# Scores of a cross-attention as three one-pass products of split operands, with the key side kept in parts for two groups of four batches and remade midway

## The chip, the cores and the metric

The kernel runs on one core of one Trainium2 chip. The metric is the time of one execution on the device in microseconds (us). Engines go by the profile's short names: PE (TensorE matmuls; PEld are its weight loads), DVE (VectorE), ACT (ScalarE), POOL (GpSimd), SP (SyncE, which issues most DMAs). A measurement of this kernel can tell about 0.2% from no change.

## The reference

One decoder layer on x of 16 batches x 256 rows x 128 features, with a context of 16 x 64 x 128. It has three parts, each followed by a residual sum and a layer norm. Cut to what matters:

```python
q, k, v = split_heads(x @ Wq + bq), ...            # 16 heads of 8
q = elu(q) + 1; k = elu(k) + 1
k = k / sqrt(sum(k * k, -1) + EPS)
attn = (q @ k^T) @ v                               # no softmax: linear
x = layernorm(x + layernorm(x + attn @ Wo + bo) * gamma + beta)

q, k, v = x @ Wq, context @ Wk, context @ Wv       # 16 heads of 64, 64 context rows
attn = softmax(q @ k^T / 8)
x = layernorm(x + (attn @ v) @ Wo)

h = silu(fp4(x) @ fp4(w_gate)^T) * (fp4(x) @ fp4(w_up)^T)   # fp4: blocks of 16, scaled to their maximum
x = layernorm(x + fp4(h) @ fp4(w_down)^T)
```

## The kernel before

**Work and tiles.** A batch is two tiles of 128 rows. For every batch the kernel runs a front (the linear attention and its two norms, which give `x1`), a cross-attention of two tiles, and an FFN. The wide intermediate results are in PSUM, whose eight banks of 512 floats a partition are shared out as `A1` and `A2` (one bank each) and `S`, `TP`, `F` (two each).

**Scores.** The query and key weights are folded: for each head h, G_h = Wk_h Wq_h^T, and M_h = G_h^T ctx^T, so that the scores of a tile are x1 M. G is made at the start and split into a part rounded to fewer bits and the rest (`GT[:, 0]` and `GT[:, 1]`, of type fp32r, which PE takes in one pass). The context is split likewise (`ctx_r`). The upper part of a split is cut with a bit mask on DVE (`context_cut`, `g_cut_high`, `gate_up_cut`, `xf_cut_high`), copied to fp32r by ACT, and the rest is a subtraction. M of all 16 heads and all 16 batches is then made in the head of the program, as 32 head products (16 heads x two halves of the batches, `m_product`) of three fp32r matmuls of 512 columns each, and kept as plain fp32 by ACT and DVE in turns (`m_keep`). The scores of a tile (`scores`) are two fp32 matmuls of 512 columns; the compiler makes two instructions of every fp32 matmul, so a tile has four.

**A tile's way.** `S` holds a tile's scores: `score_max` (DVE) takes the maxima of 16 heads, `scores_shift` (PE) subtracts them by a matmul, `softmax_exp` (ACT) writes `pe`; POOL folds halves and later multiplies by the reciprocal sums; `p_transpose` and `values` (PE) fill `TP`, ACT copies it to SBUF, and `cross_out` uses it. `x1_transpose` writes the transposed `x1` into `S` too, and `keep_x1T` (ACT) copies it out before the scores. `h_transpose` of the FFN also uses `TP`.

**Order.** There is no scheduler at run time. Each engine has its own list of calls, written out, which it takes strictly in order; semaphores hold an instruction until what it needs is there or its buffer is free. DVE's list begins with biases, masks and splits; the FFN weights are quantised in the head (`weights_max` to `weights_dequantised`, DVE) and transposed by PE (`weights_transpose`).

The products that the change is about read so in the kernel before:

```python
for n, (left, right) in enumerate(PARTS):          # m_product: 3 parts
    te.matmul(m_bank(half, hd), GT[:, left, hd, :], ctx_r[:, right, 512 * half:512 * half + 512], ...)
for half in range(2):                              # scores
    te.matmul(S[:, half * BANK:half * BANK + BANK], x1T[b % 2][:, t * P:t * P + P],
              M[:, b // BH, HC * half:HC * half + HC, b % BH * R:b % BH * R + R], ...)
```

Of the kernel before, what the change touches and what calls it, by code (L numbers as in the profile page):

```python
# [17 lines left out]
def decoder_layer(nc, x, x_t, attn_w, attn_rows, ctx_t, wq_t, wk_t, wv_t, wo_in, fw_in, out):  # L18
# [17 lines left out]
    BH = B // 2  # L36
# [22 lines left out]
    with es:  # L59
# [35 lines left out]
        M = sb("M", [P, 2, HX, BH * R])  # L95
# [12 lines left out]


        m_tail = M[:, 1, :, :].rearrange("p h n -> p (h n)")  # L110
        fw, fw_v, fw_c = (m_tail[:, HX * BH * R - (k + 1) * NW:HX * BH * R - k * NW] for k in range(3))

# [14 lines left out]
        pe_ = several("pe", NPE, [P, HX * R])  # L127
        xv = several("xv", 2, [P, T * P])
        th = sb("th", [P, T, I])
        hv = several("hv", 2, [P, T * I])  # L130
# [11 lines left out]
        x1T = several("x1T", 2, [P, T * P])  # L142
# [7 lines left out]
        xf_cut = sb("xf_cut", [P, T * P])  # L150

        xf_r = [GT[:, k, 0:2 * T, :].rearrange("p (s t) n -> p s (t n)", s=2) for k in range(2)]
# [3 lines left out]
        hT = several("hT", 2, [P, T, NK * P])  # L156
# [10 lines left out]
        fw_m, fw_s, fw_r = (hT[1][:, 0, NWB * k:NWB * k + NWB] for k in range(3))  # L167
        gu_cut = [w[:, 1, 0:I] for w in hT]

        high_bits = [w[:, 512 * k:512 * k + 512] for w in pe_ for k in range(2)]  # L170
# [37 lines left out]
        c_cut, c_high, c_low = sem("c_cut"), sem("c_high"), sem("c_low")  # L208
        g_made, g_cut, g_high, g_low = sem("g_made"), sem("g_cut"), sem("g_high"), sem("g_low")
        m_made = sem("m_made")  # L210
        m_kept = {"act": sem("m_kept_act"), "dve": sem("m_kept_dve")}
# [15 lines left out]
        x1T_made, x1T_kept, vo_made, vo_kept = sem("x1T_made"), sem("x1T_kept"), sem("vo_made"), sem("vo_kept")  # L227
# [7 lines left out]
        xf_cut_made, xf_low_made = sem("xf_cut_made"), sem("xf_low_made")  # L235
        gu_cut_made, gu_high_made, gu_low_made = sem("gu_cut_made"), sem("gu_high_made"), sem("gu_low_made")
# [15 lines left out]
        DN_OF = (A2, A1) if TILE_SUM_ON_PE else (A2, A2)  # L252
# [36 lines left out]
        M_BANKS = (F0, F1, TP0, TP1, S0, S1)  # L289

        def m_bank(half, hd):
            return M_BANKS[(HX * half + hd) % len(M_BANKS)]

# [3 lines left out]
        def _(sp):  # L297
# [27 lines left out]
            load_xT(2)  # L325
            load_x(2)
            load_xT(3)
            load_x(3)
            load_xT(4)
# [6 lines left out]
            load_x(8)  # L336
            load_xT(7)
            load_xT(8)
            load_xT(9)
            load_x(9)  # L340
            load_x(10)
            load_x(11)
            load_xT(10)
            load_xT(11)
            load_x(12)
            store_out(0)
            store_out(1)
            load_xT(12)
            load_x(13)
            store_out(2)  # L350
            load_x(14)
            load_xT(13)
            load_xT(14)
            store_out(3)
            load_x(15)
            load_xT(15)
            store_out(4)
            store_out(5)
            store_out(6)
# [9 lines left out]
            store_tile(15, 1)  # L369
            for n in range(2):  # L370
                sp.wait_ge(out_stored[n], 16 * (B // 2 + n))

        @block.gpsimd
        def _(pool):
# [28 lines left out]
            def context_low(half):  # L403
                pool.wait_ge(c_cut, half + 1)
                cols = slice(512 * half, 512 * half + 512)
                ge.tensor_tensor(ctx_r[:, 1, cols], ctx_f[:, cols], high_bits[half], ALU.subtract).then_inc(c_low, 1)

            def gate_up_low(m):
                pool.wait_ge(gu_cut_made, m + 1)
                ge.tensor_tensor(w_gu_r[:, 1, m, :], w_gu[:, m, :], gu_cut[m], ALU.subtract).then_inc(gu_low_made, 1)  # L410
# [107 lines left out]

            context_low(0)
# [3 lines left out]
            k_norm(0)  # L523
            gate_up_low(0)
            gate_up_low(1)
            minus_mean("attn", 0)
            variance_eps("attn", 0)
            rstd_of("attn", 0)
            shift_of("attn", 0)
            times_gamma(0)  # L530
            plus_x_beta(0)
            k_norm(1)
            x_plus_rows(2)
            variance_eps("post", 0)
            minus_mean("post", 0)
            rstd_of("post", 0)
            shift_of("post", 0)
            k_norm(2)
            variance_eps("attn", 1)
            minus_mean("attn", 1)  # L540
            rstd_of("attn", 1)
            shift_of("attn", 1)
# [3 lines left out]
            fold_halves(0, 0)  # L546
            minus_mean("post", 1)
            variance_eps("post", 1)
            k_norm(3)
            rstd_of("post", 1)  # L550
            shift_of("post", 1)
            probabilities(0, 0)
            variance_eps("attn", 2)
            fold_halves(0, 1)
            minus_mean("attn", 2)
            rstd_of("attn", 2)
            shift_of("attn", 2)
            probabilities(0, 1)
            times_gamma(2)
            plus_x_beta(2)  # L560
            x_plus_rows(4)
            minus_mean("post", 2)
            variance_eps("post", 2)
            fold_halves(1, 0)
            rstd_of("post", 2)
            k_norm(4)
            shift_of("post", 2)
            probabilities(1, 0)
            fold_halves(1, 1)
            variance_eps("cross", 0)  # L570
            rstd_of("cross", 0)
            minus_mean("cross", 0)
            shift_of("cross", 0)
            probabilities(1, 1)
            k_norm(5)
            fold_halves(2, 0)
            x_dequantise(0)
            variance_eps("cross", 1)
            minus_mean("cross", 1)
            rstd_of("cross", 1)  # L580
            shift_of("cross", 1)
            probabilities(2, 0)
            k_norm(6)
            fold_halves(2, 1)
            variance_eps("attn", 3)
# [3101 lines left out]
```

## Time and profile before

| | us |
|---|---|
| median of 3 runs (lowest, highest) | 372.77 (372.73, 373.13) |
| span of the profiled execution | 371.1 |
| PE busy | 349.7 (94%) |
| DVE busy | 308.7 (83%) |
| ACT busy | 253.6 (68%) |
| POOL busy | 269.0 (73%) |

The profiled execution has a span, from its first to its last instruction, of 371.1 us; the runs' median lies 1.7 us above it, which is what lies around the span. Busy time is the time in which an engine runs at least one instruction. PE's matmuls overlap at their ends, so the pace of a kind of matmul is read from the distance between the ends of successive groups, not from the mean duration of one.

### The profile page before, as it was taken

To read this page: it belongs to the slowest core of one execution; us is meant where nothing else is said; L and a number is where in the kernel's file an instruction comes from. 1 tells how busy PE (TensorE), PEld (TensorE's weight loads), DVE (VectorE), ACT (ScalarE), POOL (GpSimd) and SP (SyncE) were. 2 spreads that over 40 slices of the span, in tenths; PEclk is the share of its full clock that TensorE was granted. 3 is DMA by queue.
4 is the path that set the end of the run, shared out by engine and by line. 5 is a ranking of instruction groups with operands and counts; after the bars stand their busy time and mean duration, and the time that the engine had idled before them with its cause. 6 is when DMAs were issued, how large, how long until landed. Compare 5 with 4: busy or idle time off the path is not lost.

```text
span 371.1 us, 7329 instructions
## 1 busy us (share of the span) xinstructions
PE 349.7 (94%) x2147; PEld 267.9 (72%) x2147; DVE 308.7 (83%) x858; ACT 253.6 (68%) x533; POOL 269.0 (73%) x453
## 2 busy tenths in 40 slices
PE   8999989999998999999999999999999999998774
PEld 7788646675775868787678877786767787887653
DVE  3998557567689998869989779979998998999994
ACT  2957766577676677678688767878767666864553
POOL 4404459958988699969689895898988569784535
PEclk9999999999999999999999999999999999999999
DMA  8900100001000001000000000100000000000010
GB/s 248 305 2 16 30 1 16 14 16 29 15 17 14 17 0 44 28 18 16 29 14 17 14 1 17 31 0 0 17 15 2 15 2 1 15 16 14 3 30 28
DMA packets 13586, 10.44 MB, mean 28 GB/s; under 512 B 971, under 2 KB 12396, under 8 KB 13548
## 3 DMA queue, kind: packets, MB, share of 16 engines
q1 hardware_dynamic: 12540, 7.89, 7.1%
q10 hardware_dynamic: 1008, 2.10, 1.7%
q8 instruction: 18, 0.29, 0.3%
q14 instruction: 20, 0.16, 0.1%
HBM read 7.88 MB, written 2.10 MB: 27 GB/s over the span
## 4 chain that ended last, share of the span: by engine, by line
PE 70%; DVE 9%; POOL 8%; issue 6%; ACT 4%; DMA 1%; SPq 0%; POOLq 0%; DVEq 0%
PE A L2892 13%; PE S L2862 12%; PE TP L2852 7%; PE F L2916 6%; PE TP L2880 6%; PE A L2936 5%; PE S L2871 3%; PE A L2813 2%; PE TP L2791 2%; POOL pe L440 2%; PE F L2791 2%; PE S L2791 2%; PE TP L2925 2%; PE A L2826 2%; PE A L2821 1%
## 5 line engine op out<-in xcount | busy, mean ns | idle before, releaser
L440 POOL TENSOR_TENSOR pe<-pe,srec 128x1024 f32<-128x1024 f32 x32 | 60.9, 1904 | 9.2 <-DVE srec L1860 8.9
L2862 PE MATMUL S<-M,x1T 128*128 128x512 f32 x128 | 60.7, 597 | 1.5 <-ACT pe L1076 1.4
L2892 PEld LDWEIGHTS A<-wvoT,wqkT 128*128 128x128 f32 x480 | 56.4, 192 | 3.1 <-issue 1.8
L2892 PE MATMUL A<-wvoT,wqkT 128*128 128x128 f32 x480 | 58.0, 276 | 0.1
L434 POOL TENSOR_TENSOR fold<-pe 128x512 f32<-128x512 f32 x32 | 40.9, 1277 | 14.6 <-ACT pe L1076 14.4
L1843 DVE TENSOR_REDUCE smax<-S 128x16 fp32r<-128x1024 f32 x32 | 38.7, 1211 | 3.3 <-PE S L2862 3.1
L1076 ACT ACTIVATE pe<-S 128x1024 f32<-128x1024 f32 x32 | 32.6, 1019 | 10.6 <-PE S L2871 10.3
L1081 ACT ACTIVATE wqkT<-TP 128x1024 f32<-128x1024 f32 x32 | 32.6, 1018 | 4.3 <-PE TP L2880 4.1
L2862 PEld LDWEIGHTS S<-M,x1T 128*128 128x128 f32 x128 | 22.2, 190 | 18.3 <-issue 15.3
L2916 PE MATMUL F<-w_gu_r,GT 128*128 128x352 f32 x168 | 35.1, 344 | 0.1
L2880 PE MATMUL TP<-ident,pe 128*128 128x128 f32 x256 | 33.5, 274 | 1.6 <-POOL pe L440 0.9
L2880 PEld LDWEIGHTS TP<-ident,pe 128*128 128x128 f32 x256 | 28.8, 140 | 6.2 <-issue 3.0
L2852 PE MATMUL TP<-HW,ctx_f 128*64 128x512 f32 x128 | 31.0, 605 | 0.0
L2916 PEld LDWEIGHTS F<-w_gu_r,GT 128*128 128x128 f32 x168 | 26.9, 189 | 4.4 <-issue 3.2
L2936 PEld LDWEIGHTS A<-w_dn,hT 128*128 128x128 f32 x180 | 21.5, 192 | 6.6 <-issue 4.7
L450 POOL TENSOR_TENSOR hv<-hv,ham 128x704 f32<-128x704 f32 x15 | 20.8, 1389 | 6.1 <-DVE hv L1935 5.9
L1854 DVE TENSOR_REDUCE ssum<-fold 128x16 f32<-128x512 f32 x32 | 21.7, 677 | 4.3 <-POOL fold L434 4.2
L2936 PE MATMUL A<-w_dn,hT 128*128 128x128 f32 x180 | 23.0, 277 | 2.0 <-ACT hT L1105 2.0
L425 POOL TENSOR_TENSOR kn<-fk,ky 128x256 f32<-128x256 f32 x16 | 10.1, 631 | 20.0 <-DVE ky L1808 19.9
L418 POOL TENSOR_TENSOR xb<-x_sb,rows 128x512 f32<-128x512 f32 x16 | 20.3, 1274 | 4.2 <-DMA rows<-in_attn_rows 3.0
L2871 PE MATMUL S<-smax,ident_r 128*128 128x512 f32 x64 | 21.8, 422 | 1.7 <-DVE smax L1843 1.7
L1070 ACT ACTIVATE wvoT<-TP 128x1024 f32<-128x1024 f32 x16 | 16.4, 1022 | 6.8 <-PE TP L2852 6.8
(247 smaller groups left out, 888.2 us busy)
## 6 DMA issues: line engine op xcount, KB each, us to landing
xT<-in_x_t SPq DMA_DIRECT2D x16, 128.0 KB, 2.2
x_sb<-in_x SPq DMA_DIRECT2D x16, 128.0 KB, 2.2
out<-yf SPq DMA_DIRECT2D x15, 128.0 KB, 1.8
M<-in_fw SPq DMA_DIRECT2D x1, 560.0 KB, 11.0
wqkT<-in_wq_t ACTq DMA_DIRECT2D x2, 256.0 KB, 4.6
wqkT<-in_wk_t ACTq DMA_DIRECT2D x2, 256.0 KB, 6.1
ctx_f<-in_ctx_t ACTq DMA_DIRECT2D x2, 256.0 KB, 7.0
wvoT<-in_wv_t ACTq DMA_DIRECT2D x1, 512.0 KB, 9.4
```

Source lines behind the costliest of these rows:

```text
L434: ge.tensor_tensor(by_head(fold[n % NFO][:, :]), p4[:, :, 0, :], p4[:, :, 1, :], ALU.add).then_inc(fold_made, 1)
L440: ge.tensor_tensor(w, w, spread(srec[n % NFO][:, :], HX, R), ALU.mult).then_inc(pn_made, 1)
L1076: sc.activation(pe_[n % NPE][:, :], S[:, :], ACT.Exp, scale=SCALE).then_inc(pe_made, 1)
L1081: sc.activation(pT[n % 2], TP[:, :].rearrange("p (a n) -> p a n", a=NJ), ACT.Copy).then_inc(pT_kept, 1)
L1843: ve.tensor_reduce(smax[n % 2][:, :], by_head(S[:, :]), AX.X, ALU.max, negate=True).then_inc(smax_made, 1)
L2852: last = te.matmul(TP[par * R:par * R + R, half * BANK:half * BANK + BANK], ctx_f[:, b * R:b * R + R], HW[:, par, 4 * half:4 * half + 4, : ...
L2862: last = te.matmul(S[:, half * BANK:half * BANK + BANK], x1T[b % 2][:, t * P:t * P + P], M[:, b // BH, HC * half:HC * half + HC, b % BH * ...
L2871: last = te.matmul(S[:, half * BANK:half * BANK + BANK], ident_r[:, :], spread(smax[n % 2][:, HC * half:HC * half + HC], HC, R), start=Fal ...
L2880: last = te.transpose(TP[:, j * P:j * P + P], pe_[n % NPE][:, j * P:j * P + P], ident[:, :])
L2892: last = te.matmul(part(A2, t), pT[n % 2][:, j, :], vo[b % 2][:, j, :], start=(j == 0 and b not in SUM_ON_PE), stop=(j == NJ - 1))
L2916: last = te.matmul(bk[:, 0:I], part(xf_r[b % 2][:, left, :], t), w_gu_r[:, right, m, :], start=(n == 0), stop=(n == len(PARTS) - 1))
L2936: last = te.matmul(part(DN, t), hT[b % 2][:, t, k * P:k * P + P], w_dn[:, k, :], start=(k == 0 and b not in SUM_ON_PE), stop=(k == NK - 1))
```

## The change

The scores become three fp32r products per half tile instead of one fp32 product. For this x1T is split into two fp32r parts: `keep_x1T` (ACT) now rounds into the first, and a new `x1T_keep_low` (DVE) writes the rest, from `S`. M is kept as two fp32r parts as well: `m_keep_high` (ACT) and `m_keep_low` (DVE). That doubles its bytes, so M holds only two groups of four batches at a time; groups 0 and 1 are made in the head, groups 2 and 3 later, over the places of groups 0 and 1, once the scores of those are done. A group is made in four quarters of four heads: 12 matmuls of 256 columns fill two banks, and one copy and one subtraction of 1024 columns empty them. The bit masks are gone: the rounded copy by ACT is itself subtracted. The FFN weights' work space moves from `M` to `pe`, `hv`, `hT` and `th`. `xf_r` gets its own buffers. All lists are written anew; at the end of PE's list the filling matmuls that write nothing of use (`keep_warm`) go from 18 to 24.

```diff
-        M = sb("M", [P, 2, HX, BH * R])
+        M = sb("M", [P, 2, 2, HX, BG * R], FP32R)
...
-        x1T = several("x1T", 2, [P, T * P])
+        x1T = several("x1T", 2, [P, 2, T * P], FP32R)
...
-        M_BANKS = (F0, F1, TP0, TP1, S0, S1)
+        M_BANKS = (TP, S, F, S, F, TP, S, F) + (TP,) * 8
...
             def g_keep_high(half, par):
-                k = 2 * half + par
-                act.wait_ge(g_cut, k + 1)
-                sc.activation(g_tile(half, par)[0], high_bits[2 + k].rearrange("p (a b) -> p a b", a=4),
+                act.wait_ge(g_made, half + 1)
+                sc.activation(g_tile(half, par)[0], G_BANKS[half][par].rearrange("p (a b) -> p a b", a=4),
                               ACT.Copy).then_inc(g_high, 1)
...
-            def m_keep(half, hd):
-                act.wait_ge(m_made, HX * half + hd + 1)
-                if half == 1 and hd >= 9:
-                    act.wait_ge(fwT_made, 3)
-                sc.activation(M[:, half, hd, :], m_bank(half, hd), ACT.Copy).then_inc(m_kept["act"], 1)
+            def m_keep_high(g, q):
+                act.wait_ge(m_made, NQ * g + q + 1)
+                if g >= 2:
+                    act.wait_ge(s_made, T * BG * (g - 1))
+                sc.activation(m_part(g, q, 0), m_bank(g, q), ACT.Copy).then_inc(m_high, 1)
...
+            def m_keep_low(g, q):
+                dve.wait_ge(m_high, NQ * g + q + 1)
+                ve.tensor_tensor(m_part(g, q, 1), m_bank(g, q), m_part(g, q, 0).bitcast(FP32), ALU.subtract).then_inc(m_low, 1)
+
+            def x1T_keep_low(b):
+                dve.wait_ge(x1T_kept, b + 1)
+                ve.tensor_tensor(x1T[b % 2][:, 1, :], S[:, 0:T * P], x1T[b % 2][:, 0, :].bitcast(FP32), ALU.subtract).then_inc(x1T_low, 1)
...
-            def xf_cut_high(b):
...
             def xf_keep_low(b):
-                dve.wait_ge(xf_cut_made, b + 1)
-                ve.tensor_tensor(xf_r[b % 2][:, 1, :], A2[:, 0:T * P], xf_cut[:, :], ALU.subtract).then_inc(xf_low_made, 1)
+                dve.wait_ge(xfT_kept, b + 1)
+                ve.tensor_tensor(xf_r[b % 2][:, 1, :], A2[:, 0:T * P], xf_r[b % 2][:, 0, :].bitcast(FP32),
+                                 ALU.subtract).then_inc(xf_low_made, 1)
...
+            def m_product(g, q):
+                k = 2 * (q // 2) + 2
+                pe.wait_ge(g_high, k)
+                pe.wait_ge(g_low, k)
+                pe.wait_ge(c_high, g // 2 + 1)
+                pe.wait_ge(c_low, g // 2 + 1)
+                for a in range(QH):
+                    for n, (left, right) in enumerate(PARTS):
+                        last = te.matmul(m_bank(g, q)[:, a, :], GT[:, left, QH * q + a, :], ctx_r[:, right, BG * R * g:BG * R * g + BG * R],
+                                         start=(n == 0), stop=(n == len(PARTS) - 1))
                 last.then_inc(m_made, 1)
...
             def scores(b, t):
+                g = b // BG
                 pe.wait_ge(x1T_kept, b + 1)
-                if b % BH == 0 and t == 0:
-                    pe.wait_ge(m_kept["act"], HC * (b // BH + 1))
-                    pe.wait_ge(m_kept["dve"], HC * (b // BH + 1))
-                for half in range(2):
-                    last = te.matmul(S[:, half * BANK:half * BANK + BANK], x1T[b % 2][:, t * P:t * P + P],
-                                     M[:, b // BH, HC * half:HC * half + HC, b % BH * R:b % BH * R + R],
-                                     start=True, stop=True)
+                pe.wait_ge(x1T_low, b + 1)
+                if b % BG == 0 and t == 0:
+                    pe.wait_ge(m_high, NQ * g + NQ)
+                    pe.wait_ge(m_low, NQ * g + NQ)
+                for n, (left, right) in enumerate(PARTS):
+                    for half in range(2):
+                        last = te.matmul(S[:, half * BANK:half * BANK + BANK], part(x1T[b % 2][:, left, :], t),
+                                         M[:, g % 2, right, HC * half:HC * half + HC, b % BG * R:b % BG * R + R],
+                                         start=(n == 0), stop=(n == len(PARTS) - 1))
                 last.then_inc(s_made, 1)
```

**PE in the head.** Before, PE's list in the head is mainly products of M (`ctx_r,GT`), between which single steps of batch 0's front and the transposes of the FFN weights (`F<-ident,M`) stand:

```order
L2791 MATMUL TP<-ctx_r,GT 128x512 x6
L2799 MATMUL F<-ident,M 128x128 x3
L2791 MATMUL S<-ctx_r,GT 128x512 x3
L2826 MATMUL A<-kn,vals 128x128 x2
L2799 MATMUL F<-ident,M 128x128 x3
L2791 MATMUL S<-ctx_r,GT 128x512 x3
L2831 MATMUL A<-w_attn,kvT 128x128
```

In the changed kernel batch 0's front up to its output (`kvo,fq`) stands ahead of the first quarter of M (the row of 12):

```order
L2755 MATMUL TP<-wqkT 128x128 x8
L2806 MATMUL A<-xT,w_attn 128x256
L2811 MATMUL A<-kn,vals 128x128 x2
L2816 MATMUL A<-w_attn,kvT 128x128
L2806 MATMUL A<-xT,w_attn 128x256
L2822 MATMUL A<-kvo,fq 128x128 x2
L2776 MATMUL TP<-ctx_r,GT 128x256 x12
```

What moved: the front of batch 0 went from amid the products of M to before them, and eight quarters are left in the head of what were 32 head products.

**PE at the first quarter that is remade.** Before, PE's list in the scores of batch 4 goes from tile to tile (`S<-smax` is the shift, `TP<-ident,pe` a transposed tile, `w_gu_r` the FFN's first products):

```order
L2862 MATMUL S<-M,x1T 128x512 x2
L2899 MATMUL A<-ident,xv 128x128 x2
L2871 MATMUL S<-smax,ident_r 128x512 x2
L2880 MATMUL TP<-ident,pe 128x128 x8
L2862 MATMUL S<-M,x1T 128x512 x2
```

After the change, the second scores of batch 3 (the last that read group 0) are followed by the first quarter of group 2, in `TP`:

```order
L2850 MATMUL S<-M,x1T 128x512 x6
L2806 MATMUL A<-xT,w_attn 128x256
L2904 MATMUL F<-w_gu_r,xf_r 128x352 x6
L2776 MATMUL TP<-ctx_r,GT 128x256 x12
L2811 MATMUL A<-kn,vals 128x128 x2
L2859 MATMUL S<-smax,ident_r 128x512 x2
L2796 MATMUL A<-kv_bias_r,ones_r 128x256
L2798 MATMUL A<-w_attn,xT 128x256
```

What is new: the scores have six instructions instead of four half as fast ones, and quarters of M take turns in `TP` with `values`, the transposed tiles and the FFN's transposes. Until the next row that writes `TP` (the second quarter) there stand the rows shown here, one more pair of the last two, a `w_attn,kvT` and an `x1_transpose`.

**DVE ahead of the first maximum.** In the changed kernel the subtraction for x1T stands in DVE's list eight rows ahead of the first maximum (`smax`), with steps of other batches' fronts and a copy of `HW` (a folded value weight) between:

```order
L1737 TENSOR_TENSOR x1T<-S,x1T 128x256
L1789 TENSOR_REDUCE kss<-ksq 128x32
L1741 COPY HW<-TP 128x512
L1794 TENSOR_SCALAR ky<-A 128x32
L1832 BN_AGGR mv_attn<-stats_attn 128x2
L1833 BN_AGGR mv_attn<-stats_attn 128x2
L1799 TENSOR_TENSOR kh<-kyy,A 128x32
L1803 SCALAR_TENSOR_TENSOR ky<-A,ky 128x32
L1838 TENSOR_REDUCE smax<-S 128x16
```

Behind DVE's second maximum (of batch 0's second tile) the new list has less of the fronts left than the old one: 10 instead of 11 `fk`, 11 instead of 13 `fq`, 22 instead of 24 of each of `kh` and the later `ky`, 12 instead of 13 `kvT`, 13 instead of 14 `x<-A,xb` with their statistics. It has new there: 8 `M<-TP` and 14 `x1T<-S`; and it lacks 15 `xf_cut`.

## Rows read from the trace of the kernel before

**Rows 1.** The page: span, busy time of each engine (share) and instructions.

```profile
span 371.1 us, 7329 instructions
PE 349.7 (94%) x2147; PEld 267.9 (72%) x2147; DVE 308.7 (83%) x858; ACT 253.6 (68%) x533; POOL 269.0 (73%) x453
```

**Rows 2.** Windows: stretch, its length, busy us of each engine (instructions), clock, DMA.

```profile
0.00:58.44 58.44, 54.38 (x296) 40.39 (x296) 42.30 (x106) 36.87 (x89) 24.20 (x56) 1.00 0.31 98
...
120.00:240.00 120.00, 119.30 (x757) 92.20 (x757) 105.28 (x298) 88.53 (x184) 97.96 (x154) 1.00 0.06 19
240.00:330.00 90.00, 88.78 (x568) 69.35 (x568) 82.00 (x229) 63.12 (x125) 74.80 (x128) 1.00 0.03 9
330.00:371.10 41.10, 29.23 (x204) 25.13 (x202) 34.32 (x93) 20.64 (x42) 20.24 (x43) 0.99 0.06 17
```

**Rows 3.** The page: shares of the chain that ended last, by engine and line.

```profile
PE 70%; DVE 9%; POOL 8%; issue 6%; ACT 4%; DMA 1%; SPq 0%; POOLq 0%; DVEq 0%
PE A L2892 13%; PE S L2862 12%; PE TP L2852 7%; PE F L2916 6%; PE TP L2880 6%; PE A L2936 5%; PE S L2871 3%; PE A L2813 2%; PE TP L2791 2%; POOL pe L440 2%; PE F L2791 2%; PE S L2791 2%; PE TP L2925 2%; PE A L2826 2%; PE A L2821 1%
```

**Rows 4.** Timeline of PE: start, us, instruction, count; cross-attention output and scores.

```profile
149.80 0.60 PE L2880 MATMUL TP<-ident,pe 128*128 128x128 f32 x4
150.24 3.74 PE L2892 MATMUL A<-wvoT,wqkT 128*128 128x128 f32 x32
153.81 1.88 PE L2862 MATMUL S<-M,x1T 128*128 128x512 f32 x4
```

**Rows 5.** Timeline of PE in the head: products of M, and a bias product.

```profile
18.62 0.59 PE L2813 MATMUL A<-w_attn,xT 128*128 128x256 f32 x2
18.86 0.47 PE L2811 MATMUL A<-kv_bias_r,ones_r 128*128 128x256 f32 x1
...
25.08 1.52 PE L2791 MATMUL S<-ctx_r,GT 128*128 128x512 f32 x6
26.44 1.52 PE L2791 MATMUL F<-ctx_r,GT 128*128 128x512 f32 x6
```

**Rows 6.** PEld by line: busy, mean ns of one load, idle before.

```profile
L2791 PEld LDWEIGHTS F<-ctx_r,GT 128*128 128x128 f32 x36 | 6.5, 188 | 1.4 <-DVE GT L1730 0.2
```

**Rows 7.** DVE and ACT by line: busy us, mean ns, idle before and its releaser.

```profile
L1843 DVE TENSOR_REDUCE smax<-S 128x16 fp32r<-128x1024 f32 x32 | 38.7, 1211 | 3.3 <-PE S L2862 3.1
...
L1896 DVE TENSOR_SCALAR xf_cut<-A 128x256 int32<-128x256 int32 x15 | 6.2, 414 | 1.4 <-PE A L2899 1.2
...
L1901 DVE TENSOR_TENSOR GT<-A,xf_cut 128x256 fp32r<-128x256 f32 x15 | 6.2, 411 | 0.2
...
L1737 DVE COPY M<-F 128x512 f32<-128x512 f32 x6 | 4.1, 675 | 0.6 <-PE F L2791 0.4 <-PE F L2801 0.2
...
L1724 DVE TENSOR_SCALAR pe<-F 128x512 int32<-128x512 int32 x2 | 1.3, 682 | 0.0
L1081 ACT ACTIVATE wqkT<-TP 128x1024 f32<-128x1024 f32 x32 | 32.6, 1018 | 4.3 <-PE TP L2880 4.1
...
L974 ACT ACTIVATE M<-F 128x512 f32<-128x512 f32 x6 | 3.5, 590 | 0.8 <-PE F L2791 0.8
```

**Rows 8.** Timeline: DVE's first step on data, and the first scores to the second shift.

```profile
6.39 0.15 DVE L1704 TENSOR_SCALAR bq_col<-w_attn 128x1 f32<-128x1 f32 x1 [5.26 <-DMA rows<-in_attn_rows]
...
50.12 1.88 PE L2862 MATMUL S<-M,x1T 128*128 128x512 f32 x4
52.04 1.22 DVE L1843 TENSOR_REDUCE smax<-S 128x16 fp32r<-128x1024 f32 x1 [0.34 <-PE S L2862]
53.32 0.70 PE L2871 MATMUL S<-smax,ident_r 128*128 128x512 f32 x2 [0.20 <-DVE smax L1843]
54.06 1.02 ACT L1076 ACTIVATE pe<-S 128x1024 f32<-128x1024 f32 x1 [1.59 <-PE S L2871]
58.44 0.70 PE L2871 MATMUL S<-smax,ident_r 128*128 128x512 f32 x2
```

More of the change, by code:

```diff
@@ L358, in _ @@
             store_out(5)
+            load_x(15)
             store_out(6)
@@ new lines, in _ @@
+            project_q(3)
+            pe.wait_ge(ky_made, 9)
+            kv_outer(2)
+            pe.wait_ge(m_low, 4)
+            m_product(1, 2)
+            kv_project(2)
+            attn_out(2)
+            pe.wait_ge(fq_made, 4)
+            project_kv(4)
+            pe.wait_ge(m_low, 5)
+            m_product(1, 3)
+            pe.wait_ge(m_low, 7)
+            x1_transpose(0)
+            pe.wait_ge(m_low, 6)
+            hw_product(1)
+            pe.wait_ge(fk_made, 5)
+            project_q(4)
@@ L3084, in _ @@
+            scores(0, 0)
+            values(0)
+            scores_shift(0, 0)
+            pe.wait_ge(ky_made, 15)
+            kv_outer(3)
+            pe.wait_ge(fq_made, 5)
+            project_kv(5)
+            pe.wait_ge(pe_made, 1)
+            x1_transpose(1)
+            kv_project(3)
             pe.wait_ge(vo_kept, 1)
             values(1)
-            pe.wait_ge(ky_made, 9)
-            attn_out(1)
-            pe.wait_ge(m_kept["act"], 15)
-            pe.wait_ge(m_kept["dve"], 15)
@@ L3273, in _ @@
+            h_transpose(2)
             pe.wait_ge(yx_made, 6)
-            project_q(8)
-            pe.wait_ge(pT_kept, 12)
-            values(7)
-            pe.wait_ge(xg_made, 5)
-            kv_outer(8)
-            pe.wait_ge(fq_made, 9)
-            xf_transpose(3)
-            scores_shift(6, 0)
-            pe.wait_ge(vo_kept, 8)
-            h_transpose(2)
-            kv_project(8)
+            project_kv(10)
+            pe.wait_ge(pe_made, 13)
+            scores(6, 1)
             pe.wait_ge(hg4_made, 3)
@@ L3297, in _ @@
-            pe.wait_ge(ya_made, 9)
-            kv_outer(9)
+            values(6)
+            scores(7, 0)
+            pe.wait_ge(fk_made, 12)
+            project_q(9)
             pe.wait_ge(h_made, 7)
             gate_up(3, 1)
-            pe.wait_ge(pe_made, 14)
-            x1_transpose(7)
+            pe.wait_ge(vo_kept, 7)
+            values(7)
+            pe.wait_ge(xg_made, 6)
+            attn_out(9)
+            scores_shift(7, 0)
+            pe.wait_ge(vo_kept, 8)
+            p_transpose(6, 0)
@@ L3392, in _ @@
-            pe.wait_ge(ky_made, 39)
-            kv_outer(11)
+            pe.wait_ge(fk_made, 14)
+            down(4)
             pe.wait_ge(h_made, 13)
             gate_up(6, 1)
-            kv_project(11)
+            pe.wait_ge(yf_made, 5)
+            project_q(11)
+            pe.wait_ge(hT_kept, 5)
+            values(10)
             pe.wait_ge(pe_made, 20)
             x1_transpose(10)
-            pe.wait_ge(fk_made, 14)
+            pe.wait_ge(ky_made, 42)
+            attn_out(11)
@@ L3450, in _ @@
             pe.wait_ge(pT_kept, 22)
-            values(12)
-            pe.wait_ge(pe_made, 22)
-            x1_transpose(11)
+            h_transpose(6)
+            pe.wait_ge(pe_made, 23)
+            scores(11, 1)
             pe.wait_ge(yx_made, 11)
             down(6)
-            pe.wait_ge(x1T_kept, 12)
-            scores(11, 0)
-            pe.wait_ge(ky_made, 45)
-            kv_project(13)
+            pe.wait_ge(xg_made, 9)
+            kv_outer(14)
+            scores_shift(11, 1)
@@ L3477, in _ @@
             pe.wait_ge(hT_kept, 8)
             p_transpose(11, 0)
[L3479 to L3489 removed]
+            attn_out(14)
+            scores_shift(12, 0)
+            pe.wait_ge(xf_low_made, 10)
@@ L3512, in _ @@
-            pe.wait_ge(xf_low_made, 10)
-            down(8)
-            pe.wait_ge(x1T_kept, 14)
-            scores(13, 0)
+            pe.wait_ge(pT_kept, 24)
+            h_transpose(8)
+            scores(13, 0)
+            pe.wait_ge(h_made, 19)
+            gate_up(9, 1)
+            pe.wait_ge(hT_kept, 9)
+            values(13)
+            scores_shift(13, 0)
+            pe.wait_ge(fq_made, 16)
+            down(8)
+            pe.wait_ge(xg_made, 11)
+            kv_outer(15)
+            pe.wait_ge(vo_kept, 14)
```

3062 lines of the change are left out of this document (1474 added, 1588 removed).

## The prediction

> **What bounds the kernel now.** Begin with the busy times [rows 1]: PE is busy for 349.7 of 371.1 us, and DVE, the next, for 308.7. The chain of waits that ended last runs through PE for 70% of the span, and the scores are its second largest line with 12% [rows 3]. A mean over the whole program hides stages, so the windows come next [rows 2]. From 120 to 330 us PE is busy for 208.1 of 210 us: there its work is the time. DVE is busy for 88% of the one stretch and 91% of the other, so it is close behind. In the head, up to the second shift of the scores at 58.44 us, PE is busy for 54.4 us and DVE for 42.3. In the last 41.1 us PE is busy for 29.2, DVE for 34.3: the tail is a chain of steps of the last batches, in which PE has idle time. So what PE saves counts fully in the middle, only as far as DVE follows in the head, and little in the tail.
>
> **The pace of each matmul** is read from the ends of successive rows. The four instructions of a tile's scores end at 155.69 (153.81 + 1.88); the row ahead of them ended at 153.98: 1.71 us [rows 4]. Six fp32r products of 512 columns end at 27.96, the six before at 26.60: 1.36 us, 0.227 each [rows 5]. For 256 columns there is no row of many; one such product ends at 19.33, 0.12 behind its forerunner's 19.21 [rows 5]. Its bounds: below, 0.112, the pace of the 32 instructions that end at 153.98 after 150.40 [rows 4]; above, 0.188, the duration of one weight load [rows 6], if a row of 12 products went at the pace of its loads. I take 0.12, since loads as long stand in the 32 that go at 0.112.
>
> **PE's account.** A tile's scores fall from 1.71 to 1.36 us; 32 tiles give back 11.2. M's products were 96 x 0.227 = 21.8 us and become 192 x 0.12 = 23.0, so 1.2 more. The sum is 10.0 us less on PE. The six extra `keep_warm` matmuls (1.3 us) lie in the tail's idle time; with no idle they would cost that.
>
> Where it falls: half of M (11.5 us) is now made in the middle. So the head loses 21.8 - 11.5 = 10.3 for M and 0.7 for its two tiles. It gains about one batch's front, which the new order draws forward: two `project_q` (0.43 each, half of half a tile's fp32 scores), and at 0.112 four instructions each of `kv_outer` and `attn_out` and two of `kv_project`, together 2.0. The head thus has 9.0 us less for PE; the rest has 30 x 0.35 = 10.5 less for scores, 11.5 more for M, 2.0 less of front: 1.0 less.
>
> **DVE's account.** Removed are 16 copies of M at 0.675 (10.8), 15 FFN masks at 0.414 (6.2) and eight masks in the head, six of 512 columns at 0.68 and two smaller, about 5.0 [rows 7]. Added are 16 subtractions of 1024 columns for M and 16 of 256 for x1T. The second kind is the same operation as L1901, 0.411 each, 6.6 in all. For the first no row exists; the nearest, by size and bank, is the maximum over 1024 columns, 1.21, and two copies of 512, 1.35, bound it above [rows 7]. I take 1.21: 19.4. The net is 4.0 more. Behind the second shift it is 8 x 1.21 + 14 x 0.411 - 6.2 and less one front of some 15 short steps (about 4, an estimate from steps of 0.15 to 0.5): 5.3 more. In the head it is 1.3 less, so 41.0. ACT gets 16 copies of 1.02 for 16 of 0.59, 6.9 more [rows 7]; at 68% busy it has the room. POOL's and SP's work stays as it is; the FFN weights only land in another tile.
>
> **The head, step by step.** With 9.0 us less PE would be busy for 45.4 us. DVE begins at 6.39 [rows 8] and needs 41.0: it can't reach its second maximum's end before 47.4. It had 9.8 us idle between 6.39 and 58.44, in which it waited for ACT and PE; if it keeps all of that, the second shift starts at 57.2. Part of it stays, since the rsqrt steps of the fronts (`kh`, `ky`) go to and fro between ACT and DVE whatever PE does, and new waits come: a quarter of M goes PE, ACT, DVE, and x1T waits for ACT and then DVE. Behind `x1T_keep_low` in DVE's queue stand `kss`, `HW`, a `ky` chain and the maximum, so a late `keep_x1T` holds all those, and then PE's shift and ACT's exponential. I take the middle, 53.0: **5.4 us less**, with bounds of 1.2 and 11.0.
>
> **The rest.** PE has 1.0 us less. Each remade quarter holds `TP` until ACT's copy (1.02) and DVE's subtraction (1.21) are through. Three hand-overs come to it, each 0.05: PE's scores end at 52.00, the maximum starts at 52.04 and ends at 53.26, the shift starts at 53.32 and ends at 54.02, the exponential starts at 54.06 [rows 8]. Six products last 1.52 at a pace of 1.36 [rows 5], so the last is ready 0.16 late. Together 2.54 us. What PE has to do meanwhile, behind the first of them: `kv_outer` 0.45, the shift 0.45, `project_kv` 1.10, `kv_project` 0.22, the transposes 0.22, together 2.44. So 0.1 is missing; for eight quarters I take **1.2**, with bounds of nothing and of 9.7 (DVE comes one 1.21 us step late each time, as its list is strictly in order). DVE's 5.3 us more I cost at nothing: from 240 to 330 it is 91% busy while PE stands still for only 1.2 of 90 us [rows 2], and 5.3 over some 310 us lifts its share by under 2%. DVE also has 13 steps more behind its last maximum; that work has moved from before it and adds nothing to the sum, but the last scores must come earlier by as much.
>
> **The sum.** 371.1 - 5.4 - 1.0 + 1.2 = 365.9 us of span. The runs' median lies 1.7 above the profiled span, so 367.6.
>
> **Rivals.**
> *PE's saving in full.* If DVE's waits in the head go with PE's work, all 10.0 us come out: 361.1 + 1.7 = 362.8. For it speaks the middle, where PE alone decides; against it that the head would be DVE's at 47.4 without a single wait.
> *Given back.* DVE keeps its waits in the head (1.2 gained), the remade quarters cost 1.2, and a quarter of DVE's 5.3 us more shows in the rest (1.3): 371.1 - 1.2 - 1.0 + 1.2 + 1.3 = 371.4, so 373.1, no change. DVE's 91% speaks for it, PE's nearly idle-free middle at that share against it.
> *Slower by the remade quarters.* Place: `m_keep_low` of groups 2 and 3 in DVE's list. If DVE gets there one long step late each time, PE waits ahead of the next writer of `TP`, and the transposed tiles, `values` and `h_transpose` behind it. At 9.7 us the sum is 371.1 - 5.4 - 1.0 + 9.7 = 374.4, so 376.1; from 0.8 us a quarter on it is slower than before. For it: the cover is 0.1 short already. Against: only eight places.
> *Slower by weight loads.* The 192 products of 256 columns go at the loads' 0.188: 13.1 us more, of which the head's half finds PE's idle time but for 0.5. The result is 367.6 + 0.5 + 6.5 = 374.6. Against it stands that 32 instructions, each with a load, ended every 0.112 us [rows 4]. The Trainium skill, "TensorE: Matmul & The Clock Gate", Part 3, states that a weight load overlaps running matmuls only where it targets another group of rows, which would put every load beside its product. By that rule this case would be the likely one, and 374.6 its least time; the trace of these full 128-row loads doesn't agree, as products of 0.227 with loads of 0.188 between them leave no room for it.
>
> **Chances and range.** The forecast, with 365 to 370.5 as its own range: 0.50. The full saving: 0.24. Given back: 0.12. The remade quarters: 0.11. The loads: 0.03. Leaving out the far ends of the first and the fourth, 361.5 to 374 remains. What a measurement can tell from no change is about 0.2%, 0.7 us. Of "given back" some 0.03 falls below that; so faster 0.77, same 0.09, slower 0.14.
>
> **What would show it.** Right, if six score products end 1.36 us apart from the row ahead, 12 of M take 1.4 to 1.5, `M<-TP` on DVE has a mean near 1.21, and the second shift starts at 51 to 55 us. The first step falls if that shift stands past 57 or before 50. The second falls if PE idles ahead of rows that write `TP`, released by DVE's `M`, for more than 3 us in all. The forecast is wrong altogether if PE's busy share in the middle drops below 96%, since DVE's load was then not free.

## The result and the profile after

The changed kernel takes 360.97 us (median of five runs, 360.79 to 362.69), against 372.94 for the kernel before beside it: a ratio of 0.969 [0.9672, 0.9708], 12.0 us less. In a second comparison it took 361.1 us, ratio 0.9685 [0.9669, 0.9702]. The forecast was 367.6 with a range from 361.5: the kernel is faster than the range allowed.

It was profiled twice. The first profiled execution (span 360.9) was the longest of its five; the others have spans of 359.0 to 359.5. The second has 359.4, like these, and its rows are read here. First the page's busy times and the shares of the chain that ended last, for [rows 1, 3]:

```profile
span 359.4 us, 7621 instructions
...
PE 340.4 (95%) x2319; PEld 286.7 (80%) x2319; DVE 307.9 (86%) x851; ACT 255.9 (71%) x533; POOL 272.1 (76%) x453
...
PE 35%; POOL 25%; issue 22%; DVE 11%; ACT 4%; DMA 1%; POOLq 0%; ACTq 0%; DVEq 0%
```

Next the windows of the same execution, cut at its own second and last shift of the scores (53.68 and 314.77), for [rows 2]:

```profile
0.00:53.68 53.68, 45.55 (x315) 37.28 (x316) 41.65 (x107) 38.89 (x93) 30.79 (x62) 1.00 0.35 111
53.68:120.00 66.32, 65.75 (x435) 54.40 (x434) 51.13 (x158) 48.89 (x105) 58.94 (x90) 1.00 0.05 15
120.00:240.00 120.00, 119.16 (x808) 100.48 (x806) 106.71 (x295) 90.24 (x185) 92.39 (x144) 1.00 0.05 15
240.00:314.77 74.77, 74.77 (x529) 65.03 (x527) 70.03 (x189) 54.81 (x104) 65.51 (x110) 1.00 0.04 10
314.77:359.40 44.63, 35.18 (x243) 29.50 (x241) 38.39 (x106) 23.05 (x47) 24.52 (x51) 0.97 0.07 21
```

PE is busy for 45.55 us of the head; the forecast said 45.4. The middle looks as full as before. Where the time went is read from the shifts on PE's timeline. The first fence is of the kernel before (its second shift, at 58.44, stands in [rows 8]), the other of the changed kernel:

```profile
330.02 0.60 PE L2871 MATMUL S<-smax,ident_r 128*128 128x512 f32 x2
```

```profile
50.71 1.65 PE L2850 MATMUL S<-M,x1T 128*128 128x512 f32 x6 [0.70 <-DVE x1T L1737]
...
53.68 0.70 PE L2859 MATMUL S<-smax,ident_r 128*128 128x512 f32 x2
...
314.77 0.68 PE L2859 MATMUL S<-smax,ident_r 128*128 128x512 f32 x2
```

| stretch | before, us | after, us | difference | forecast |
|---|---|---|---|---|
| start to second shift | 58.4 | 53.7 | -4.7 | -5.4 |
| second to last shift | 271.6 | 261.1 | -10.5 | |
| last shift to end | 41.1 | 44.6 | +3.5 | |
| both behind the second shift | 312.7 | 305.7 | -7.0 | +0.2 |

The head came nearly as forecast. The miss lies behind it: 7.0 us less where nothing was expected. What went is read from windows: first of the kernel before (the row that [rows 2] leave out, and the whole stretch behind the second shift), then of the changed kernel:

```profile
58.44:120.00 61.56, 58.03 (x328) 40.84 (x329) 44.80 (x136) 44.46 (x96) 51.85 (x75) 1.00 0.06 16
...
58.44:371.10 312.66, 295.34 (x1852) 227.53 (x1852) 266.40 (x753) 216.76 (x445) 244.85 (x397) 1.00 0.05 15
```

```profile
53.68:359.40 305.72, 294.86 (x2006) 249.40 (x2004) 266.26 (x745) 216.99 (x441) 241.36 (x392) 0.99 0.05 15
```

PE is busy there for 0.5 us less (295.3 to 294.9). Its idle time, the stretch less the busy time, fell by 6.5 (17.32 to 10.86):

| PE's idle time | before, us | after, us |
|---|---|---|
| second shift to 120 us | 3.5 | 0.6 |
| 120 us to last shift | 1.9 | 0.8 |
| last shift to end | 11.9 | 9.4 |
| together | 17.3 | 10.9 |

### The profile page after: what moved, and what is told of

It is laid out like the page before. It is cut to its first block, busy times and chain, and to the rows that moved or that the text cites. A ratio compares the mean times of both kernels' runs of the same rounds, so it can differ in the third digit from the quotient of the medians.

```text
span 360.9 us, 7621 instructions
## 1 busy us (share of the span) xinstructions
PE 342.2 (95%) x2319; PEld 288.1 (80%) x2319; DVE 307.8 (85%) x851; ACT 256.0 (71%) x533; POOL 271.8 (75%) x453
## 4 chain that ended last, share of the span: by engine, by line
PE 52%; POOL 16%; issue 14%; DVE 11%; ACT 4%; DMA 1%; POOLq 0%; ACTq 0%; DVEq 0%
PE A L2880 11%; PE S L2850 8%; PE TP L2837 5%; PE TP L2868 5%; PE F L2904 4%; POOL pe L445 3%; PE A L2798 3%; PE A L2924 2%; PE S L2859 2%; POOL fold L439 2%; PE TP L2776 2%; POOL hv L455 2%; DVE smax L1838 2%; PE TP L2913 2%; DMA wqkT<-in_wk_t 1%
## 5 line engine op out<-in xcount | busy, mean ns | idle before, releaser
L2850 PE MATMUL S<-M,x1T 128*128 128x512 f32 x192 | 52.8, 410 | 0.7 <-DVE x1T L1737 0.7
L439 POOL TENSOR_TENSOR fold<-pe 128x512 f32<-128x512 f32 x32 | 42.1, 1314 | 12.6 <-ACT pe L1081 12.4
L2850 PEld LDWEIGHTS S<-M,x1T 128*128 128x128 f32 x192 | 34.0, 189 | 10.4 <-issue 1.8
L1086 ACT ACTIVATE wqkT<-TP 128x1024 f32<-128x1024 f32 x32 | 32.7, 1021 | 10.9 <-PE TP L2868 10.8
L2904 PE MATMUL F<-w_gu_r,xf_r 128*128 128x352 f32 x168 | 33.9, 337 | 0.1
L2904 PEld LDWEIGHTS F<-w_gu_r,xf_r 128*128 128x128 f32 x168 | 27.4, 188 | 1.4 <-DVE h L1899 0.5
L1849 DVE TENSOR_REDUCE ssum<-fold 128x16 f32<-128x512 f32 x32 | 21.3, 672 | 6.1 <-POOL fold L439 6.0
L430 POOL TENSOR_TENSOR kn<-fk,ky 128x256 f32<-128x256 f32 x16 | 11.1, 696 | 16.9 <-DVE ky L1803 16.7
L2859 PE MATMUL S<-smax,ident_r 128*128 128x512 f32 x64 | 21.4, 416 | 0.7 <-DVE smax L1838 0.7
```

The source lines that it names most:

```text
L439: ge.tensor_tensor(by_head(fold[n % NFO][:, :]), p4[:, :, 0, :], p4[:, :, 1, :], ALU.add).then_inc(fold_made, 1)
L1086: sc.activation(pT[n % 2], TP[:, :].rearrange("p (a n) -> p a n", a=NJ), ACT.Copy).then_inc(pT_kept, 1)
L2850: last = te.matmul(S[:, half * BANK:half * BANK + BANK], part(x1T[b % 2][:, left, :], t), M[:, g % 2, right, HC * half:HC * half + HC, b % ...
L2859: last = te.matmul(S[:, half * BANK:half * BANK + BANK], ident_r[:, :], spread(smax[n % 2][:, HC * half:HC * half + HC], HC, R), start=Fal ...
L2904: last = te.matmul(bk[:, 0:I], part(xf_r[b % 2][:, left, :], t), w_gu_r[:, right, m, :], start=(n == 0), stop=(n == len(PARTS) - 1))
```

## Experiments

Each kernel was run in three rounds beside the kernel before (372.65 to 372.99 in these comparisons). Differences below are from the before of the same comparison. Theory A is that PE's work decides and what it saves counts in full. Theory B is that each engine's strictly ordered list is fitted to durations, that a chain of hand-overs runs right behind PE, and that the new lists made the gain.

**1. The new products in the old lists.** x1's second part is subtracted on DVE (16 times); the part of M that doesn't fit is read from other heads' places.

```diff
+            x1T_keep_low(0)
...
+                pe.wait_ge(x1T_low, transposed[0])
+                for n, (left, right) in enumerate(PARTS):
+                    for half in range(2):
+                        last = te.matmul(S[:, half * BANK:half * BANK + BANK], part(x1T[b % 2][:, left, :], t),
...
+                                         start=(n == 0), stop=(n == len(PARTS) - 1))
-                for half in range(2):
-                    last = te.matmul(S[:, half * BANK:half * BANK + BANK], x1T[b % 2][:, t * P:t * P + P],
```

> The lists of before, with the scores as three one-pass products and x1T's subtraction put into DVE's list where ACT's copy of x1T had ended in the trace of before. M is rounded to one part and made whole in the head as before; the scores take its upper part twice (M's rest is left out), and for the second eight batches heads 9 to 15 are read from other heads' places. Theory A (the gain is PE's work, every us of it, and DVE's 6.6 us more are free): 32 x 0.35 = 11.2 us less, 361.7 us. Theory B (the new lists are what saved waits; old lists can't use the shorter scores): 365 us or more. Theory C (shorter scores take waits away too, as the way of a tile through S gets shorter): 360 us or less.

372.35 us, 0.9993 [0.9984, 1.0003]: no gain that can be told from none, as Theory B expected. Its page's busy times, its chain, and two of PE's waits:

```profile
PE 345.5 (93%) x2211; PEld 280.3 (76%) x2211; DVE 311.7 (84%) x874; ACT 254.2 (69%) x533; POOL 269.6 (73%) x453
...
POOL 37%; issue 24%; PE 21%; DVE 13%; ACT 3%; POOLq 1%; DVEq 0%; ACTq 0%
```

```profile
PE S L2900 <- DVE smax L1851: 2.9, 6, 1.1
...
PE S L2891 <- DVE x1T L1846: 1.6, 5, 0.6
```

By the forecast's paces PE has 11.2 us less to do, but its busy time fell by only 4.2 (349.7 to 345.5) and the time by 0.3. PE fell out of the chain (70% to 21%): it now waits for the others. Its idle time rose by 3.9 (21.4 to 25.3); the other 7 us of the 10.9 that it waits longer don't show as idle time.

**2. The old products in the new lists.** The subtractions for the second parts still run.

```diff
-                for n, (left, right) in enumerate(PARTS):
-                    for half in range(2):
-                        last = te.matmul(S[:, half * BANK:half * BANK + BANK], part(x1T[b % 2][:, left, :], t),
-                                         M[:, g % 2, right, HC * half:HC * half + HC, b % BG * R:b % BG * R + R],
...
+                for half in range(2):
+                    last = te.matmul(S[:, half * BANK:half * BANK + BANK], part(x1T[b % 2][:, 0, :], t),
+                                     M[:, g % 2, 0, HC * half:HC * half + HC, b % BG * R:b % BG * R + R],
```

> The changed kernel with its own lists, M and x1T kept as plain fp32 copies, and the scores again one fp32 product of four instructions; DVE's subtractions still run (they write zeros that nothing reads). Theory A: 11.2 us more than the changed kernel, 372.2 us. Theory B: less than 11.2 more, 368 us or less, since the new lists have waits in which PE's extra work fits. Theory C: more than 11.2, 374 us or more.

370.64 us, 0.9946 [0.9931, 0.9960]: 9.7 above the changed kernel, between Theories A and B and nearer A. Here the same 11.2 us of PE's work count almost fully.

**3. The new lists without the remade quarters.** The eight quarters of groups 2 and 3 are left out, and those groups' scores read the M of groups 0 and 1.

```diff
-            m_product(2, 0)
...
-            m_keep_high(2, 0)
...
-            m_keep_low(2, 0)
```

> The changed kernel without the eight remade quarters: products, copies and subtractions of groups 2 and 3 are left out, and batches 8 to 15 take their scores from the M of batches 0 to 7. PE has 96 products of 256 columns less, 11.6 us; DVE 9.7 us less, ACT 8.2 less. Theory A: 349.4 us. If the quarters also made PE wait for TP (the recorded forecast took 1.2 us for it): 348 us. If DVE was a bound in the middle after all: below 347 us.

358.28 us, 0.9613 [0.9599, 0.9628], 2.7 less than the changed kernel: all three expectations fail. By the rows' paces PE has 11.5 us less to do, DVE 9.8, ACT 8.2. But behind the second shift PE now stands idle for 18.7 us instead of 10.9. Taking work out of lists that were written for it frees little, as in experiment 1, so this run doesn't show what the quarters cost where they stand.

**4. Only the FFN mask left out of the kernel before.**

```diff
-            xf_cut_high(0)
...
-                dve.wait_ge(xf_cut_made, b + 1)
-                ve.tensor_tensor(xf_r[b % 2][:, 1, :], A2[:, 0:T * P], xf_cut[:, :], ALU.subtract).then_inc(xf_low_made, 1)
+                dve.wait_ge(xfT_kept, b + 1)
+                ve.tensor_tensor(xf_r[b % 2][:, 1, :], A2[:, 0:T * P], xf_r[b % 2][:, 0, :].bitcast(FP32),
+                                 ALU.subtract).then_inc(xf_low_made, 1)
```

> The kernel before with one part of the change alone: the FFN's mask on DVE is gone, ACT rounds straight from PSUM and DVE subtracts that. DVE has 15 x 0.414 = 6.2 us less, and its subtraction now waits for ACT's copy. Theory A: no change, 372.9 us within 0.7. If DVE's load was a bound in the old lists: 2 to 6 us less. If the wait for ACT holds up what is queued behind it: 1 to 3 us more.

377.01 us, 1.0114 [1.0097, 1.0131]: DVE is busy for 5.4 us less and the kernel is 4.4 us slower, more than the third expectation's 1 to 3. DVE's largest wait is one that the kernel before doesn't have, for ACT's copy of the same 256 columns:

```profile
DVE GT L1895 <- ACT GT L1093: 12.0, 13, 1.9
```

**5. The same, with the subtraction one to six steps later in DVE's list**, in twelve of 15 batches (its expectation counts eleven and five).

```diff
-            xf_keep_low(0)
             score_max(3, 0)
+            xf_keep_low(0)
```

> The kernel before without the FFN mask (which alone gave 377.0, with 12.0 us of DVE's waiting for ACT at the subtraction of 256 columns behind it), and with that subtraction moved back in DVE's list by one to five steps in eleven of 15 batches, so that the steps behind it need not wait. If the 4.4 us came from its place in the list: 371.5 to 373.5, so the loss goes. If they came from the longer way of the FFN's input itself (PE, ACT, then DVE): 375.5 to 378.

384.17 us, 1.03 [1.0271, 1.0329], 11.3 us slower than the kernel before: both expectations fail. DVE's wait fell from 12.0 to 1.1, but PE's FFN products now wait for DVE:

```profile
PE F L2896 <- DVE GT L1895: 6.9, 4, 1.7
```

Neither the old place nor these later ones suit the step. Whether it would be free if its neighbours on PE and ACT moved too was not tried.

**6 and 7. POOL's longest step halved**, with the old and with the new products in the old lists; **8, below,** does it in the changed kernel.

```diff
-                w = by_head(pe_[n % NPE][:, :])
-                ge.tensor_tensor(w, w, spread(srec[n % NFO][:, :], HX, R), ALU.mult)
+                w = by_head(pe_[n % NPE][:, :])[:, 0:HX // 2, :]
+                ge.tensor_tensor(w, w, spread(srec[n % NFO][:, 0:HX // 2], HX // 2, R), ALU.mult)
```

> The kernel before, with the multiplication of the probabilities (POOL, 1.90 us, 32 times) done on half of its columns only; the other half stays without its division, so the output isn't the reference's. POOL has about 30 us less, and each tile's probabilities come some 0.95 us sooner. Theory A (PE's work is the time of this kernel, POOL has slack): no change, 372 to 373. Theory B (a chain through POOL, DVE and ACT stands right behind PE): little or no change here either, since PE's 349.7 us of work stay; at most 2 us less. A fall of 5 us or more would say that PE's 70% of the chain of waits was misleading in the kernel before.

> The lists of before with the new products of the scores (which alone gave 372.35) and with POOL's multiplication of the probabilities on half of its columns, as in the run beside it. Theory B1 (the 11.3 us that PE saves were lost to the chain of hand-overs in which POOL has 37%): with POOL's step shorter a good part of the saving shows, 363 to 367. Theory B2 (the old lists themselves hold it, each engine waiting at places that POOL does not decide): 370 to 373, as with POOL's full step. Theory A expects what it expected of the new products alone, about 362.

372.33 us (0.9982 [0.9972, 0.9991]) and 370.22 us (0.9928 [0.9913, 0.9943]). POOL's busy time falls by 27 us in both (269.6 to 242.2 in the second), and the second gains 2.3 on experiment 1, relative to its own before. The first is what Theories A and B both expected. The second lies in the range of B2, and B1 fails: POOL's 37% of the chain are not a price, and this step of POOL is not what holds most of the saving.

**8.** 

> The changed kernel with POOL's multiplication of the probabilities on half of its columns (as done with the lists of before, where it gave 0.5 us with the old products and 2.1 with the new). If POOL's chain (16% of the chain of waits after the change) is what the changed kernel is next held by: 356 to 359. If its lists keep PE supplied in spite of POOL: 360 to 361.5.

360.55 us, 0.9671 [0.9657, 0.9685]: as the changed kernel, within 0.2%, so its lists keep PE supplied in spite of POOL.

**9. The new products in the old lists, without x1's subtractions.**

```diff
-            x1T_keep_low(0)
...
-                        last = te.matmul(S[:, half * BANK:half * BANK + BANK], part(x1T[b % 2][:, left, :], t),
+                        last = te.matmul(S[:, half * BANK:half * BANK + BANK], part(x1T[b % 2][:, 0, :], t),
```

> The lists of before with the new products of the scores, but without the 16 subtractions on DVE that make x1's second part (the products read the first part twice, so the output isn't the reference's; PE's work is the same). Tells whether those 6.6 us on DVE, with a wait for ACT ahead of each, ate the saving. If they did: 362 to 366. If the old lists hold it: 370.5 to 372.5.

368.26 us, 0.9873 [0.9858, 0.9888], between the two expectations. The subtractions, 6.6 us of DVE, ate 4.3 us at the places where experiment 1 put them (the difference of -0.3 and -4.6); of PE's 11.2 the old lists still keep more than half. Its shifts on PE:

```profile
58.30 0.70 PE L2883 MATMUL S<-smax,ident_r 128*128 128x512 f32 x2 [0.41 <-DVE smax L1851]
...
325.31 0.59 PE L2883 MATMUL S<-smax,ident_r 128*128 128x512 f32 x2
```

Between the two lie 267.0 us, only 4.6 less than before, though 30 tiles lie there.

**10 and 11. The new lists without all 32 subtractions**, with the new and with the old products. The edit is that of experiment 9, with `m_keep_low` left out as well.

> The changed kernel without the 32 subtractions on DVE that make the second parts of M and x1 (some 26 us of DVE; the products read the first parts twice, so PE's work is the same and the output isn't the reference's). Tells what the subtractions cost in the new lists; with the lists of before, leaving out the 16 of x1 alone gave back 4.1 us (372.35 to 368.26). If the new lists hide them: 359.5 to 361.5, with the second shift of the scores still near 55 us. If DVE is what the changed kernel waits for: 351 to 357. Whichever way, a second shift at 51 to 53 us would show that they are what the head waits for.

> The changed kernel's lists with the old products of the scores (which gave 370.64 with the subtractions still in DVE's list), now without the 32 subtractions (some 26 us of DVE). PE's work, about 333 us, is then nearly that of the kernel before. If the orders alone remove waits and the subtractions are hidden: 369.5 to 371. If the subtractions cost as much as those of x1 did in the lists of before, or more: 363 to 367.

359.48 us (0.9644 [0.9629, 0.9658]) and 369.16 us (0.9903 [0.9886, 0.9919]). In the new lists some 26 us of DVE's subtractions cost 1.9 and 1.8 us (the second against experiment 2); in the old ones 6.6 us cost 4.3. Both times lie just under the range for hidden subtractions. The second shift of experiment 10 came at 52.6, which its expectation took as a sign that the head waits for them; counted from DVE's first step it is only 0.5 us sooner than in the changed kernel (46.4 against 46.9).

**12. The changed kernel once more.**

> The changed kernel itself, once more with a profile. Its first profiled execution (span 360.9) was the longest of its five, the others have spans of 359.0 to 359.2, and its second shift of the scores starts at 55.3 us; with POOL's multiplication shortened, which touches nothing ahead of the first shift, it started at 53.1, and the 2.2 us between the two stand in the first 15 us, where DVE waits for its first row of weights to land. If the late landing is the whole of it: span near 359, second shift at 53.0 to 53.7, so the head would be as forecast (53.0) and all that was missed lies behind it. If the changed kernel's head is really longer than the forecast's: second shift past 54.5 again.

361.1 us, with the second shift at 53.68: the head is as forecast. From each one's second shift to its end, the two profiled executions agree (305.7 us both). They part twice in the head. DVE's first step waits 0.83 us longer for its weights to land in the first, and PE is then late by as much (its row at 11.74 against 10.91). Behind that, from 12 to 15 us, the first execution's granted clock is 0.51 (the lower of PE's two levels, 1.2 and 2.4 GHz) where the second has 1.00, and PE is 1.58 late (15.79 against 14.21). The second execution and then the first, each with the window from 12 to 15 us between its timeline rows:

```profile
6.75 0.15 DVE L1712 TENSOR_SCALAR bq_col<-w_attn 128x1 f32<-128x1 f32 x1 [5.61 <-DMA rows<-in_attn_rows]
...
10.91 0.39 PE L2796 MATMUL A<-kv_bias_r,ones_r 128*128 128x256 f32 x1 [1.30 <-DVE fk L1779]
...
12.00:15.00 3.00, 2.07 (x20) 1.27 (x18) 1.58 (x7) 2.49 (x9) 0.47 (x1) 1.00 1.08 382
...
14.21 0.70 PE L2806 MATMUL A<-xT,w_attn 128*128 128x256 f32 x2 [0.84 <-DVE fk L1779]
```

```profile
7.58 0.15 DVE L1712 TENSOR_SCALAR bq_col<-w_attn 128x1 f32<-128x1 f32 x1 [6.45 <-DMA rows<-in_attn_rows]
...
11.74 0.39 PE L2796 MATMUL A<-kv_bias_r,ones_r 128*128 128x256 f32 x1 [1.29 <-DVE fk L1779]
...
12.00:15.00 3.00, 3.00 (x16) 2.17 (x17) 0.99 (x4) 1.61 (x7) 0.00 (x0) 0.51 1.09 387
...
15.79 0.70 PE L2806 MATMUL A<-xT,w_attn 128*128 128x256 f32 x2
...
55.25 0.70 PE L2859 MATMUL S<-smax,ident_r 128*128 128x512 f32 x2
```

So the late landing is about half of the 1.57 us between the two second shifts. Whether it also brought the clock down isn't shown.

The experiments split the result in three, each difference against its own before:

| step | us |
|---|---|
| new lists, old products, no subtractions (experiment 11) | -3.8 |
| new products in them (10 less 11) | -9.7 |
| the 32 subtractions (12 less 10) | +1.9 |
| together | -11.6 |

The same new products, also without subtractions, gave 4.6 in the old lists. So of the 11.6 us some 5.1 (9.7 - 4.6) are a saving of PE that only the new lists can use, and 3.8 come from the new lists with the rest of the change (M remade, masks gone), although M's products alone cost PE 1.2 us more there.

## Why the prediction was wrong, point by point

**Paces: right.** Twelve products of M take 1.43 us (they end at 96.73 + 1.59 = 98.32, the row ahead at 96.41 + 0.48 = 96.89), where 1.4 to 1.5 was forecast. Six products of the scores take 1.43 (109.55 less 108.12), where 1.36 was, so a tile saves 0.28 to 0.35:

```profile
96.41 0.48 PE L2904 MATMUL F<-w_gu_r,xf_r 128*128 128x352 f32 x2
96.73 1.59 PE L2776 MATMUL TP<-ctx_r,GT 128*128 128x256 f32 x12
```

```profile
107.08 1.04 PE L2868 MATMUL TP<-ident,pe 128*128 128x128 f32 x8
107.90 1.65 PE L2850 MATMUL S<-M,x1T 128*128 128x512 f32 x6
```

The rival of the weight loads fell with the first of these. The Trainium skill's rule behind it ("TensorE: Matmul & The Clock Gate", Part 3) would add each load's time to its product's; at 0.12 us a product, with loads of 0.19 between them, these rows don't agree with it.

**The subtractions on DVE: right.** M's take 1.22 us (1.21 taken), x1's 0.41:

```profile
L1733 DVE TENSOR_TENSOR M<-TP,M 128x1024 fp32r<-128x1024 f32 x10 | 12.2, 1222 | 0.8 <-ACT M L979 0.7
L1737 DVE TENSOR_TENSOR x1T<-S,x1T 128x256 fp32r<-128x256 f32 x16 | 6.5, 406 | 0.6 <-ACT x1T L1071 0.6
```

Costing DVE's extra load at nothing was nearly right too, in lists that had been made for it: experiments 1 and 9 show that x1's step is dear where it was put into the old list. The forecast's 4.0 us more for DVE can't be seen in its busy time (308.7 to 307.9), which counts steps that overlap once; the durations of DVE's rows, added up, rise from 355.2 to 360.4.

**The head: right.** 53.7 us against 53.0, inside its mark of 51 to 55; the 55.25 of the first execution is outside it for the reasons given in experiment 12. (The middle between 47.4 and 57.2, which the forecast says it takes, is 52.3, not 53.0.) The wait foreseen for x1T is there (0.70 ahead of the scores at 50.71).

**The remade quarters: no wait to speak of.** The waits that the profile lists for PE from the second to the last shift come to 1.1 us, and none of them is for DVE's M. The rival "slower by the remade quarters" fell. What the quarters cost in all stays open (experiment 3).

**The rest: wrong, and this is the step that failed.** Behind the second shift the forecast books 1.0 us less of PE's work and 1.2 more of its waits, +0.2 in all; measured is -7.0. The work was about right: PE is busy for 0.5 us less. The waits went the other way: PE's idle time fell by 6.5 us, from 17.3 to 10.9, where 1.2 more was booked. From 120 to 330 us PE's "work is the time" indeed, with 1.9 us idle, but the forecast let that stretch stand for the whole rest. Most of the 17.3 us lay outside it: 3.5 ahead of 120 us, in a stretch whose row it leaves out, and 11.9 behind the last shift, where it expected little to change; there PE is now busy for 6.0 us more in a stretch only 3.5 us longer. The sum takes these waits as given and has no term for what new lists do to them.

That the new lists took them out, and not the shorter products, is shown by experiments 2 and 1, whose windows from the second shift to the end are these:

```profile
53.88:368.40 314.52, 303.68 (x1946) 238.54 (x1944) 267.30 (x745) 217.65 (x441) 241.08 (x392) 1.00 0.05 14
```

```profile
58.47:370.80 312.33, 291.01 (x1912) 238.55 (x1912) 269.92 (x768) 217.34 (x445) 245.38 (x397) 1.00 0.05 15
```

The new lists with the old products leave PE idle for 10.8 us, as the changed kernel does; the old lists with the new products leave it idle for 21.3.

Idle time need not be all of PE's waiting. A product's row lasts 275 ns in the changed kernel, while 32 of them end every 112 ns before [rows 4], so a gap of up to 0.16 us between two starts can be covered by the earlier row:

```profile
L2880 PE MATMUL A<-wvoT,wqkT 128*128 128x128 f32 x480 | 57.3, 275 | 0.0
```

The 7 us of experiment 1 that don't show fit such gaps, but no row shows one. For the change itself they aren't needed: 6.5 us of idle time and 0.5 of busy time make up the 7.0. The forecast's own alarm, a busy share below 96% in the middle, watched for more waits only and could not tell of fewer.

**The rivals.** "PE's saving in full" came nearest, with 362.8, but not by its mechanism: it put the gain into the head, which gave 4.7. "Given back" names about the time of the old lists in experiment 1 (373.1 against 372.35), but its reason, waits of DVE in the new lists' head and at the quarters, isn't theirs. No version here that does all the work beats the changed kernel. Which of the new lists' moves took the waits out stays open; the lists were only tried as a whole, with M remade and the masks gone.

## What to carry to other kernels

Strictly ordered lists on several engines are fitted to the durations that they were written for. Cheaper work put into the old lists may give nothing (11.2 us of PE's work gave 0.3) and even lose (a mask less: 4.4 us slower), so a change of durations that comes with new lists has to be forecast together with them. A busy share near 100% in one stretch doesn't bound what new orders can give in the others: add up the bottleneck engine's idle time over the whole program (17.3 us behind the second shift here), keep it as a possible gain in the range, and read the rows of every stretch. The other way round, less work need not show as idle time (experiment 1). A cost is known only for the list in which it stands; the same step was dear in one and nearly free in the other.

## What was not expected of the hardware

The chain's shares are no property of a kernel. Two executions of the changed kernel, 1.5 us apart, show PE with 52% and 35% and POOL with 16% and 25%; here is the first one's, for the line shown above:

```profile
PE 52%; POOL 16%; issue 14%; DVE 11%; ACT 4%; DMA 1%; POOLq 0%; ACTq 0%; DVEq 0%
```

And two executions of one kernel can differ in their first 15 us: by 0.83 us in the landing of the first weights (DVE's first step at 6.75 and 7.58), and in PE's granted clock (1.00 and 0.51 from 12 to 15 us, after PE had been busy for 3.8 and 3.2 of the 6 us ahead). The second shift then differs by 1.57, and the time by 1.5.
